# A gated attention and MLP block on one core: narrow values by batch, searches from the fourth slot, four buffers of exponentials

## The reference

```
xn  = layernorm(x)                                  # x: (4, 1024, 256) float32
qkv = xn @ w_qkv                                    # 16 heads of 16
s   = softmax(causal(q k^T / 4)) v @ w_out
y   = xn
for i in range(6):
    y = gelu(y @ W1[i].T + B1[i]) @ W2[i].T + B2[i] + y     # exact gelu, 1024 hidden
    if i < 5: y = layernorm(y) * LN_G[i] + LN_B[i]
out = x + s * silu(y)
```

## Time and profile before

| what | us |
|---|---|
| median of three runs | 1791.66 |
| the profiled execution's own time | 1795.63 |
| its span from first to last instruction | 1793.9 |
| PE busy, share of span | 1657.8 (92%) |
| DVE / ACT / POOL busy | 1156.0 / 871.8 / 297.6 |
| DMA moved | 150.26 MB, 84 GB/s over the span |

### The profile page before, as it was taken

The page is one execution under the profiler, slowest core; times in us unless marked ns, Lnnn a source line. Parts: engine busy times, 40 slices in busy tenths (PEclk is TensorE's granted clock), DMA queues, the critical chain, the costliest instruction groups (busy, mean ns, idle before and its releaser), DMA issues. The chain is left out here.

```text
span 1793.9 us, 29506 instructions
## 1 busy us (share of the span) xinstructions
PE 1657.8 (92%) x11216; PEld 1341.4 (75%) x11216; DVE 1156.0 (64%) x2924; ACT 871.8 (49%) x1220; POOL 297.6 (17%) x274
## 2 busy tenths in 40 slices
PE   6967999999999999999999999999999998889736
PEld 6856888898888888888888888899995443334236
DVE  6715777777776777777777777765554565556036
ACT  3432444444444344444444444344446887779713
POOL 1020111111111111111111111111111222222214
PEclk9978999999999999999999999999998998899869
DMA  8978224243020020300200202032003666554313
GB/s 271 330 215 191 79 84 108 64 120 85 13 42 22 13 48 7 57 13 11 44 14 21 43 13 48 2 97 36 2 1 67 162 163 153 150 150 128 89 57 138
DMA packets 90504, 150.26 MB, mean 84 GB/s; under 512 B 10560, under 2 KB 66368, under 8 KB 84096
## 3 DMA queue, kind: packets, MB, share of 16 engines
q1 hardware_dynamic: 90368, 148.44, 31.7%
HBM read 113.53 MB, written 60.03 MB: 97 GB/s over the span
## 5 line engine op out<-in xcount | busy, mean ns | idle before, releaser
L589 ACT ACTIVATE m_hid<-m_h_ps,m_b1s 128x512 f32<-128x512 f32 x384 | 264.2, 688 | 718.6 <-PE m_h_ps L687 684.3
L650 DVE TENSOR_TENSOR m_hidl<-m_hid,m_hidh 128x512 fp32r<-128x512 f32 x384 | 288.4, 751 | 276.3 <-ACT m_hidh L592 275.3
L843 ACT ACTIVATE a_prob<-a_st_ps 128x1024 f32<-128x1024 f32 x288 | 278.7, 1022 | 59.3 <-PE a_st_ps L881 54.6
L700 PE MATMUL m_y_ps<-shared,m_hidh 128*128 128x256 f32 x1536 | 284.9, 283 | 11.2 <-DVE xres L606 11.2
L687 PE MATMUL m_h_ps<-m_xth,shared 128*128 128x512 f32 x768 | 277.0, 402 | 5.0 <-DVE m_xtl L601 2.4
L700 PEld LDWEIGHTS m_y_ps<-shared,m_hidh 128*128 128x128 f32 x1536 | 248.4, 189 | 26.0 <-DVE m_hidl L650 11.4
L567 POOL TENSOR_TENSOR xres<-xres,m_b2s 128x1024 f32<-128x1024 f32 x48 | 132.6, 2763 | 805.0 <-DVE xres L606 805.0
L592 ACT ACTIVATE m_hidh<-m_h_ps,m_b1s 128x512 fp32r<-128x512 f32 x384 | 260.9, 679 | 0.0
L700 PE MATMUL m_y_ps<-w2h,m_hidh 128*128 128x256 f32 x768 | 216.8, 282 | 0.0
L700 PE MATMUL m_y_ps<-shared,m_hidl 128*128 128x256 f32 x768 | 216.1, 281 | 0.0
L700 PE MATMUL m_y_ps<-w2l,m_hidh 128*128 128x256 f32 x768 | 214.1, 279 | 0.0
(11 more groups left out here) (113 smaller groups left out, 2693.8 us busy)
## 6 DMA issues: line engine op xcount, KB each, us to landing
shared<-q_stacks SPq DMA_DIRECT2D x32, 400.0 KB
shared<-k_stacks SPq DMA_DIRECT2D x32, 400.0 KB
q_stacks<-q_parts SPq DMA_DIRECT2D x96, 128.0 KB
k_stacks<-k_parts SPq DMA_DIRECT2D x96, 128.0 KB
mk<-k_stacks SPq DMA_DIRECT2D x32, 384.0 KB, 10.7
mq<-q_stacks SPq DMA_DIRECT2D x22, 384.0 KB, 5.5
q_parts<-mq SPq DMA_DIRECT2D x16, 512.0 KB, 3.9
k_parts<-mk SPq DMA_DIRECT2D x16, 512.0 KB, 5.1
```

Of the source, the lines that this page charges most:

```text
L589: nc.scalar.activation(hid[n % 2][:], h_ps[n % 2][:], ACT.Gelu, bias=b1s[i % 2][:, k:k + 1])
L650: nc.vector.tensor_tensor(hidl[n % 4][:], hid[n % 2][:], hidh[n % 4][:].bitcast(F32), ALU.subtract).then_inc(low_done, 1)
L700: m = nc.tensor.matmul(y_ps[:, j, :], h[n % 4][:, j * P:(j + 1) * P], w[par][:, k, :], start=(k == 0 and j % 2 == 0 and h is hidh and w is ...
L843: nc.scalar.activation(to, scores, ACT.Exp).then_inc(exp_done, 1)
```

## The change

Values are stored once per batch, 256 wide and without ones (`vd` becomes [4, 128, 8, 256]), in one DMA per token group. They are loaded per batch into the two `apart` tiles of the search, now kept through the attention stage as `vb`; POOL copies a group's 4 heads from there into `va`, which holds the ones from the start. The last token group's q and k are stored in mlp instead of at the end of project. The search has `AHEAD` = 11 groups (230 visits) in mlp, starts in the fourth slot and takes chunks 1 to 6, and its first loads move from before the weights of slot 0 to slot 1. The attention stage has four `prob` tiles and values three steps behind. x is no longer loaded whole during the attention stage but by pair, beside the attention output, in the combine stage.

```diff
-AHEAD = 10
+AHEAD = 11
...
+def load_values(sp, scratch, keep, bt):
+    sp.dma_start(keep["vb"][(AHEAD + bt) % 2], scratch["v"][bt]).then_inc(keep["v_loaded"][bt % 2], 16)
+def augment(nc, pool, keep, n):
+    bt, hg = divmod(n, HG)
+    pool.wait_ge(keep["v_loaded"][bt % 2], 16 * (bt // 2 + 1))
+    values = keep["vb"][(AHEAD + bt) % 2][:, :, HG * HD * hg:HG * HD * (hg + 1)].rearrange("p t (h d) -> p t h d", d=HD)
+    nc.gpsimd.tensor_copy(keep["va"][n % 2][:, :, :, 0:HD], values).then_inc(keep["v_ready"], 1)
...
# project, SP
-                for hg in range(HG):
-                    values = vout[g % 2][:, :, HG * hg:HG * (hg + 1), :].rearrange("p j h d -> p j (h d)")
-                    sp.dma_start(vd[HG * bt + hg, :, first:first + TILES, :], values).then_inc(v_stored[g % 2], 16)
+                store_values(g)
...
+            sp.wait_ge(v_copied, GROUPS)
+            store_values(GROUPS - 1)
             for u in range(2):
-                sp.wait_ge(v_stored[u], 16 * HG * PAIRS)
-                for m in range(4):
-                    sp.wait_ge(part_stored[u][m], 16 * PAIRS)
+                sp.wait_ge(v_stored[u], 16 * PAIRS)
...
# mlp
+        FROM = 3
         for v in range(VISITS):
-            slot, place = divmod(2 * v, 9)
-            AT.setdefault(CH * (1 + slot) + (1, 4, 4, 5, 5, 6, 6, 7, 7)[place], []).append(v)
+            n = 6 * (SLOTS - FROM) * v // VISITS
+            AT.setdefault(CH * (FROM + n // 6) + 1 + n % 6, []).append(v)
...
+            for m in range(4):
+                store_part(sp, scratch, keep, GROUPS - 1, m)
             for n in range(2):
                 lay_out_stacks(sp, scratch, keep["ones"], n, keep["laid"])
-            sp.wait_ge(keep["laid"], 2 * LAYING * 16)
-            sp.wait_ge(cleared, 6)
-            for m in range(2):
-                search.load(sp, m)
             for t in range(SLOTS + 1):
...
+                if t == 1:
+                    sp.wait_ge(keep["laid"], 3 * LAYING * 16)
+                    sp.wait_ge(cleared, 6)
+                    for m in range(2):
+                        search.load(sp, m)
...
+                        if m == AHEAD - 2:
+                            load_values(sp, scratch, keep, 0)
...
# mlp, POOL: first waits for the stored parts; at its end
+            for n in range(2):
+                augment(nc, pool, keep, n)
...
-BUFS = 3
-LATE = 2
+BUFS = 4
+LATE = 3
...
# attend, SP
+            load_values(sp, scratch, keep, 1)
...
                 if step == 0:
-                    load_rows(n)
...
                 if step == 3 and n:
-                    sp.wait_ge(av_done, NS * n)
-                    if n + 1 < N_GROUPS:
-                        load_values(sp, scratch, keep, n + 1)
                     store_o(n - 1)
+                    bt = n // HG + 1
+                    if n % HG == 0 and 2 <= bt < BATCH:
+                        sp.wait_ge(keep["v_ready"], n)
+                        load_values(sp, scratch, keep, bt)
...
# attend, POOL
+                if step == 5 and n and n + 1 < N_GROUPS:
+                    pool.wait_ge(av_done, NS * n)
+                    augment(nc, pool, keep, n + 1)
...
# combine: in load_pair; PE waits for both, POOL adds xt
+    sp.dma_start(keep["xt"][c][:], x[bass.ds(P * i, 2 * P), :].rearrange("(t p) d -> p t d", p=P)).then_inc(keep["ot_loaded"][c], 16)
```

More of the change, by code:

```diff
@@ L245, in project @@
         gtl = [b.sb(f"p_gtl{u}", [P, HALVES, GT], F32R) for u in range(2)]
-        part = [[keep[n][u][:, PARTS * GT * v:PARTS * GT * (v + 1)].rearrange("p (a n) -> p a n", a=PARTS)
-                 for n in ("mq", "mk") for v in range(2)] for u in range(2)]
-        vout = [b.sb(f"p_vout{u}", [P, TILES, HEADS, 2 * HD]) for u in range(2)]
+        part = [[part_tile(keep, u, m) for m in range(4)] for u in range(2)]
+        vout = [b.sb(f"p_vout{u}", [P, TILES, DIM]) for u in range(2)]
         stats = [b.sb(f"p_stats{u}", [P, TILES, 6]) for u in range(2)]
@@ L263, in project @@
         qk_done, part0_done, part1_done = b.sem("p_qk_done"), b.sem("p_part0_done"), b.sem("p_part1_done")
-        part_stored = [[b.sem(f"p_part_stored{u}{m}") for m in range(4)] for u in range(2)]
+        part_stored = keep["part_stored"]
+        v_stored = [b.sem(f"p_v_stored{u}") for u in range(2)]
         v_done, v_copied = b.sem("p_v_done"), b.sem("p_v_copied")
-        v_stored = [b.sem(f"p_v_stored{u}") for u in range(2)]
         ident_ready, half_ready = b.sem("p_ident_ready"), b.sem("p_half_ready")
@@ L286, in _, with store_values @@
                 load_x(g)
-            for g in range(GROUPS):
+            def store_values(g):
+                first = TILES * (g % 2)
+                sp.dma_start(scratch["v"][g // 2, :, first:first + TILES, :], vout[g % 2][:]).then_inc(v_stored[g % 2], 16)
+            for g in range(GROUPS - 1):
                 for m in range(4):
                     sp.wait_ge(part1_done, 4 * g + m + 1)
-                    rows = (qd if m < 2 else kd)[P * (m % 2):P * (m % 2) + P]
-                    sp.dma_start(rows[:, :, GT * g:GT * (g + 1)], part[g % 2][m].bitcast(F32)).then_inc(part_stored[g % 2][m], 16)
+                    store_part(sp, scratch, keep, g, m)
                 sp.wait_ge(v_copied, g + 1)
-                bt, first = g // 2, TILES * (g % 2)
-                for hg in range(HG):
-                    values = vout[g % 2][:, :, HG * hg:HG * (hg + 1), :].rearrange("p j h d -> p j (h d)")
-                    sp.dma_start(vd[HG * bt + hg, :, first:first + TILES, :], values).then_inc(v_stored[g % 2], 16)
+                store_values(g)
                 if g + 2 < GROUPS:
@@ L536, in _ @@
                     load_bias(i + 1)
+                if t == 1:
[3 more added lines that the diff above has]
+                        search.load(sp, m)
+                if t + 2 == N_GROUPS - HG:
+                    for m in range(4):
+                        sp.wait_ge(keep["part_stored"][1][m], 16 * PAIRS)
                 if t + 2 < N_GROUPS:
@@ L551, in _ @@
                         load_stacks(sp, scratch, sq[n], sk[n], n, keep["qk_loaded"][n])
-                        load_values(sp, scratch, keep, n)
             for n in range(2):
                 sp.wait_ge(keep["qk_loaded"][n], LOADS * 16)
-                sp.wait_ge(keep["v_loaded"][n], 16)
         @block.gpsimd
         def _(pool):
+            for u in range(2):
+                for m in range(4):
+                    pool.wait_ge(keep["part_stored"][u][m], 16 * PAIRS)
             for stack in (*search.q, *search.apart, *search.k):
@@ L995, in body @@
                 nc.gpsimd.tensor_tensor(res[c][:, t, :], res[c][:, t, :],
[L996 removed]
+                                        keep["xt"][c][:, t, :], ALU.add).then_inc(added, 1)
             steps(pool, (0,), body)
@@ L1087, in gated_block @@
         b = Bufs(nc, ctx)
+        apart = [b.sb(f"apart{u}", [P, PAIR * SEQ], F32R) for u in range(2)]
         shared = [b.sb(f"shared{n}", [P, HALVES * HID], F32R) for n in range(4)]
@@ L1113, in gated_block @@
             project(nc, x, wqkv, w1t, w2t, scratch, keep)
-            search.apart = stack_views([b.sb(f"x_apart{u}", [P, PAIR * SEQ], F32R) for u in range(2)])
+            search.apart = stack_views(apart)
             mlp(nc, w1t, w2t, b1, b2, ln_g, ln_b, scratch, keep, search)
         b = Bufs(nc, ctx)
-        keep |= {"x": b.sb("x_rows", [P, TOK // P, DIM]), "rows_loaded": b.sem("rows_loaded")}
         keep |= {
@@ L1122, in gated_block @@
             "ot": [b.sb(f"ot{c}", [HG * (HD + 1), HG, 2 * P]) for c in range(OT)],
+            "xt": [b.sb(f"xt{c}", [P, 2, DIM]) for c in range(OT)],
             "ot_loaded": [b.sem(f"ot_loaded{c}") for c in range(OT)],
@@ L1125, in gated_block @@
         attend(nc, x, wout, scratch, keep, search)
-        combine(nc, out, scratch, keep)
+        combine(nc, x, out, scratch, keep)
 def kernel(L0_attn_x, L0_attn_w_qkv, L0_attn_w_out, L0_ffn_W1, L0_ffn_B1, L0_ffn_W2, L0_ffn_B2, L0_ffn_LN_G, L0_ffn_LN_B):
```

42 lines of the change are left out of this document (19 added, 23 removed).

## The result

The kernel after takes 1765.74 us in the median of four runs (1762.98 to 1768.20); the kernel before, on the same chip, 1790.49 (1788.26 to 1793.19). The ratio is 0.9861, with a 95% interval of 0.9839 to 0.9882. The gain is 24.8 us, and the forecast of 1753 us had promised 38 against its median, so two thirds of it came; the time is inside the range of 1736 to 1778.

What follows compares the result with a forecast made beforehand. The prediction took PE to bound mlp and ACT's exponentials to bound attention, with 55 us of holes, mostly late loads. Terms summed to -39.3 us, 1756.3 against 1795.6; less 4.0 for the median, forecast 1753, range 1736 to 1778.

Steps and rivals of the forecast that it cites:

- rival 2: Combine: x costs its whole time, queueing at the pair loads' engines; chain +11, tail +6, total 1765 us; chance 0.14.
- end of project: Before mlp: one value store in place of four lets SP keep up; mlp starts at 97.4, gain 9.7 us.
- slots 0 and 1, place and layer ends: Mlp: no early wait for weights, -14.8 us; visits beside DVE's work in chunk 3, +5; five layer ends, +2.4.
- 21 more visits: Mlp: twenty more search visits at 0.48 us each and a small one, +9 us taken.
- attend: Attention stage: fewer bytes queued leave 17 us of 55 us of holes in ACT's exponentials, gain 38; bounds 12 and 48.
- combine: Last stage: x loaded beside each pair lengthens the chain through pair loads, +5 us; bounds +1 and +11.
- chunks with visits rise above 3.8 us: Mlp: a sign that, if seen, would make the forecast wrong.
- 9 of late loads: Attention stage: the part of the 17 us of remaining holes put down to late loads, 9 us.
- The rival of holes that stay: Attention stage: per-group stores are untouched and traffic only a fifth less, so gain 12 there, 1779 us; chance 0.12.
- four links of the chain at +1.2: Combine: 256 KB more per pair lengthens four links of the chain of pair loads by 1.2 us each, +5.
- 4 x 0.4 us of issue: Tail: SP's issue time for four x loads now ahead of the last stores, within a term of +0.5 us.
- early stall: Mlp, slots 0 and 1: waiting for late weights; a rival had q and k stores bring it back, +12, 1765; chance 0.05.

Runs made afterwards that it cites:

- e4: Kernel before with the late searches alone (first search loads in slot 1 behind the weights, visits in chunks 1 to 6 from the fourth slot): 1779.07 us, ratio 0.993.
- e10: Kernel before with late searches, attention stores as 16 rows and one, and combine's attention-output loads as 64 rows and four: 1708.49 us, ratio 0.9537.
- e5: Kernel before with only its attention stores changed, each of 17 rows cut into one of 16 rows and one of one row: 1733.64 us, ratio 0.9678.
- e6: Kernel after with ten groups of searches ahead in mlp instead of eleven: 1759.97 us, ratio 0.9824.
- e7: Kernel after with ten groups of searches ahead and attention stores as 16 rows and one: 1719.28 us, ratio 0.9601.
- e3: Kernel after with each attention store of 17 rows cut into one of 16 rows and one of the last row: 1729.47 us, ratio 0.9653.
- e11: e9 with nine groups of searches ahead in mlp instead of ten: 1735.68 us, ratio 0.9687.
- e9: e7 with the attention output laid out so that combine loads it as 64 rows and four instead of 68: 1701.32 us, ratio 0.9504.
- e1: Kernel after with three tiles of exponentials and values two steps behind, instead of four and three: 1764.34 us, ratio 0.9829.
- e2: Kernel after without the 16 loads of x in combine, adding normalized x from SBUF instead (output lacks x): 1753.52 us, ratio 0.9784.

## Why the prediction was right, point by point

The sum was -39.3 us against the profiled execution; -27.4 came, between profiled executions. The time lies in the range, but the forecast itself (1756.3 less 4.0 is 1752.3, put down as 1753) was 13 us too low, a third of the gain that it promised. The measured 1765.7 is the number of rival 2, though not by its mechanism.

| term | forecast | measured | from |
|---|---|---|---|
| end of project | -9.7 | -12.2 | mlp starts at 94.9 |
| slots 0 and 1, place and layer ends | -14.8 + 5 + 2.4 | -17.1 and -13.3 | e4's mlp; e10's against e5's |
| 21 more visits | +9 | +10.5 to +14.8 | e6; e7 against e3; e11 against e9 |
| end of mlp, and what is left of mlp | +1.3 | +3, within what mlp differs by | e6 against e4 |
| attend | -38 | -29.1 | table |
| tail | +0.5 | +1.6 | table |
| combine | +5 | +11.3 | table |

*End of project.* SP is no longer behind, as argued; how much of it the narrow values give and how much the moved q and k stores is open. I had put the start of mlp 2.5 us later: ACT's last copy ended 1.0 earlier, the issue took 0.33 instead of 1.15, and the barrier 2.8 instead of 3.5.

*Mlp.* The total, +0.8, is near the +2.9 of the sum, but two terms were off and cancelled, which is luck. Chunk 4 is slower as argued (3.75), but a chunk 7 of 2.8 pays for it, and e4 and e10 leave nothing to 2 us of the 7.4. The sign that "chunks with visits rise above 3.8 us" was badly put: chunk 2 with a visit has 4.16, since it had 3.69 without one. A visit's price of 0.43 (9 us by 21) came from a single pair of chunks; as a whole group it is 0.5 to 0.7. Why it is more isn't shown; that in slots as full as these another visit waits for the reduction before it would fit.

*Attend.* The step that failed is "9 of late loads": the two late groups and their restarts take 15.0 of the 26.3 us of waits for scores (4.41, 1.56 and 0.27; 5.69, 1.57 and 1.48). The small holes were put too low as well, at 5: 0.15 at every fourth of 288 exponentials is 10.8, and some 9 came. Half the relief was there, as two groups instead of four begin late, but a search load and 1 MB of values in one DMA still meet the slow stores, and 13.8 us of PE's waits are for stacks. The reading behind the step, one busy engine that everything else queues behind, fits, and the slow stores weigh more than I had made them: without them attend is 290.5 us. The rival of holes that stay (forecast 1779) was wrong by as much on the other side.

*Combine.* The "four links of the chain at +1.2" came out as PE's waits for loads, which grew by 5.2 us. What failed is that the sum had nothing else in this stage: PE was busy 6.0 longer for the same matmuls at a clock of 0.79 instead of 0.90. So the upper bound of 11 came, but not as rival 2 had it, with the chain alone longer by the whole load. In the tail, where rival 2 had +6, 1.6 came. There "4 x 0.4 us of issue" was wrong: the four x loads took SP 18.5 us to issue, but the four pair loads beside them 2.3 instead of 17.5.

*The rest.* The early stall didn't return, and DVE did not become mlp's bound (890.9 us busy of 1257.8). The fourth buffer is worth nothing (e1). Whether a copy on GpSimd holds up a VectorE instruction can't be read from any run by itself, but there is no sign of the 9 us that the prediction named as possible: with ten groups ahead and spread stores, attend is 295.3 us with 14 such copies (e7) and 298.2 with none (e5).

## What to carry to other kernels

Look first for a window in which one kind of DMA runs alone: its GB/s and DMA share tell on how many engines it goes (0.07 is about one in sixteen), and a store of 17 rows here slowed everything behind it. Had the row of 26 GB/s been taken as the thing to mend and not as the surroundings of the change, one edit of three lines would have given 59 us where this change gave 25. Fillers on the engines that feed the pace-setter (here PE and DVE, which feed ACT) have a count at which they turn from cheap to dear: up to one visit a step cost attend 5 to 8 us a group, the second in a step 2 us each.

## What was unexpected of the hardware

A DMA of 16 rows and one of a single row, issued one after the other, are far cheaper than one of 17 rows: 128 DMAs in place of 64 for the same bytes took 59 us off the kernel before. Likewise 64 rows and four rows in place of 68 took 11 us off combine (e10 against e5, where PE's waits for loads fell from 12.0 to 0.7).

TensorE's granted clock made up half of what the loads of x cost in combine, and the idle tail ahead of the stage doesn't explain it. In every profile the first 5 us of combine are at 0.50 (1.2 GHz), after a tail of 7.6 us (e9, e10) as after one of 29.3 (e1), and from 10 to 15 us in the clock is at 1.00 (2.4 GHz). The kernels differ in whether it falls again behind that: from 15 to 20 us in it is 0.66 before and in e3, but 1.00 in e2, e5, e9 and e10. The first 20 us of the kernel before, of e3 and of e2, behind tails of 25.8, 11.4 and 25.0 us (these windows mix the two levels):

```profile
1729.10:1749.00 19.90, 16.26 (x111) 15.33 (x112) 13.67 (x39) 8.21 (x21) 5.12 (x7) 0.68 0.21 69
```

```profile
1649.60:1669.00 19.40, 14.85 (x99) 13.91 (x100) 12.29 (x35) 7.52 (x19) 4.37 (x6) 0.68 0.25 77
```

```profile
1682.70:1702.00 19.30, 13.92 (x106) 12.65 (x106) 13.40 (x39) 8.20 (x21) 5.22 (x8) 0.80 0.21 68
```

A tail half as long left the clock as low, and a long one was followed by a higher clock. What decides isn't shown: in the 5 us ahead of the second fall PE is busy 3.95 us in the kernel before, and in e2, where no fall follows, 3.18.

Issuing a single DMA took SP up to 12.63 us in attend (the load of 1 MB of values at 1513.76 after) and 8.66 (the x load at 1652.50), with slow stores issued ahead of both, where single issues elsewhere take as little as 0.3 to 0.4.
